# Mixing 64x64 token blocks in the corners of TensorE, with its place and the projection's last quarter reordered

## The reference

```python
# attention, last line: the heads' outputs o go through Wo
return jnp.einsum('bto,do->btd', o, Wo)

# the mixing: x is (batch, token c, feature t); w is one of eight 64x64 matrices
w = weights[subjects]
b = bias[subjects]
out = jnp.einsum('bct,bcd->bdt', x, w)
out = out + b[:, :, None]

x = x + _L2_cond_ref(...)      # x3 in the kernel
x = x + _L3_cond_ref(...)      # x4 in the kernel, the output
```

## Time and profile before

| | us |
|---|---|
| median of 3 runs | 908.46 |
| lowest and highest | 903.56, 910.40 |
| profiled execution, its own time | 904.41 |
| its span in the trace | 902.6 |

### The profile page before, as it was taken

One profiled execution on the slowest core, in us unless ns is written; L12 is line 12 of the kernel. 1 busy time (PEld: TensorE's weight loads), 2 busy tenths in 40 slices (PEclk: granted clock), 3 DMA queues, 4 the chain that ended last, 5 costly groups with the idle time before them and its releaser, 6 DMA issues. The chain is left out here.

```text
span 902.6 us, 23448 instructions
## 1 busy us (share of the span) xinstructions
PE 874.2 (97%) x6451; PEld 654.3 (72%) x6451; DVE 651.3 (72%) x1832; ACT 439.8 (49%) x1161; POOL 525.8 (58%) x496
## 2 busy tenths in 40 slices
PE   6899999999999999999996999999999999999997
PEld 4466676676767667667675788888888888888885
DVE  4664456788777855477666688888888888888885
ACT  2433333333433334333333666766667666676663
POOL 2146556566565658865558666666666666666630
PEclk9999999999999999999997999999999999999999
DMA  9999987988879788888554666666676686666741
GB/s 314 351 342 356 348 278 258 308 273 273 278 263 310 270 292 274 271 277 293 206 198 133 202 212 212 187 199 216 194 221 191 203 245 201 202 204 204 242 130 49
DMA packets 99985, 218.45 MB, mean 242 GB/s; under 512 B 29755, under 2 KB 35736, under 8 KB 91746
## 3 DMA queue, kind: packets, MB, share of 16 engines
q1 hardware_dynamic: 65858, 145.17, 48.7%
q0 software_dynamic: 25088, 57.74, 20.9%
q10 hardware_dynamic: 8992, 15.00, 4.5%
HBM read 210.29 MB, written 33.86 MB: 271 GB/s over the span
## 5 line engine op out<-in xcount | busy, mean ns | idle before, releaser
L618 POOL DMA_INDIRECT ring<-new_rows,idx x128 | 130.8, 1022 | 101.5 <-DVE big L1617 79.9
L1164 ACT ACTIVATE big<-big,neg_max 128x320 f32<-128x320 f32 x256 | 141.7, 560 | 6.3 <-DVE neg_max L1588 1.9
L1588 DVE CUSTOM_DVE_ANT_0 big<-banks,mask 128x320 f32<-128x320 f32 x256 | 114.8, 486 | 14.8 <-PE banks L878 10.8
L663 PE MATMUL banks<-ring 128*64 128x512 f32 x512 | 117.2, 600 | 3.9 <-DMA ring<-in_w 3.9
L1154 ACT ACTIVATE kt<-banks 128x384 f32<-128x384 f32 x128 | 62.6, 489 | 109.2 <-PE banks L856 109.1
L543 POOL TENSOR_TENSOR rms<-ss,neg_half 128x12 f32<-128x12 f32 x29 | 66.4, 2289 | 66.5 <-DVE ss L1494 66.5
L878 PEld LDWEIGHTS banks<-kt,q_in 64*128 64x128 f32 x768 | 75.1, 191 | 23.5 <-issue 11.6
L878 PE MATMUL banks<-kt,q_in 64*128 64x128 f32 (+2 forms) x768 | 89.0, 365 | 2.9 <-ACT kt L1154 1.3
L1617 DVE TENSOR_SCALAR big<-big,recip 128x320 f32<-128x320 f32 x256 | 84.8, 393 | 2.3
L1013 ACT ACTIVATE pair_b_hi<-pair_b,reals 128x512 fp32r<-128x512 f32 x32 | 23.2, 726 | 124.3 <-DMA pair_b<-in_lb 124.1
L541 POOL TENSOR_TENSOR ring<-ring 128x512 f32<-128x512 f32 x29 | 37.6, 1297 | 72.5 <-DVE ring L1360 72.5
(11 more groups left out here) (191 smaller groups left out, 1979.7 us busy)
## 6 DMA issues: line engine op xcount, KB each, us to landing
ring<-in_w SPq DMA_DIRECT2D x62, 1024.0 KB, 8.0
ring<-in_xt SPq DMA_DIRECT2D x32, 256.0 KB, 2.8
x_in<-in_x SPq DMA_DIRECT2D x32, 256.0 KB, 5.7
bias_in<-in_b SPq DMA_DIRECT2D x64, 128.0 KB, 8.2
x_dram<-x SPq DMA_DIRECT2D x32, 256.0 KB, 9.0
q_dram<-q_t ACTq DMA_DIRECT2D x32, 256.0 KB, 6.9
q_in<-q_dram SPq DMA_DIRECT2D x32, 256.0 KB, 2.9
x_in<-x_dram SPq DMA_DIRECT2D x32, 256.0 KB
```

What stands on the lines that cost most here:

```text
L618: pool.indirect_dma_start(out=kv[:, s, c, :], out_offset=None, in_=new_rows, in_offset=bass.IndirectOffsetOnAxis(ap=idx[:, b, 1 + c:2 + c] ...
L663: last = nc.tensor.matmul(ps_l0[T * h:T * h + T, :], xt[:, s, c, T * h:T * h + T], w0[:, 2 * s + h, c * D:(c + 1) * D], start=(c == 0), st ...
L1164: nc.scalar.activation(prob[:, s % 2, PLACE[g] * NK:(PLACE[g] + 1) * NK], sm[:, s % 2, g, :], ACT.Exp, bias=neg_max[:, s % 2, g:g + 1], sc ...
L1588: V.tensor_tensor_reduce(sm[:, s % 2, g, :], ps_s[g], mask[:, s % 2, k0:k0 + NK], 1.0, 3.0e38, ALU.add, ALU.min, accum_out=neg_max[:, s % ...
```

## The change

The mixing becomes four matmuls of 64x64 by 256 columns, one in each corner of the array: token half h of the pair (rows) times column half i. `bd` keeps one 64x64 matrix per batch, with no zeros, and DVE adds an identity to it (`join_identity`), so that the matmul gives x3 plus the mixing. DVE's `add_x4` goes; ACT adds the bias in two ACTIVATEs of 128x256 (`add_bias`), after `ot_hi` in the odd step. The four results lie in rows 64i of two banks, `ps_x` for h = 0 and the second half of bank 6 for h = 1. `mix()` moves from ahead of the values to behind `own_values()`. The projection is turned to go over chunks inside products; three chunks stay in the odd step and the last moves to the even step, ahead of the values. `add_x3` moves from the start of DVE's even step to where `add_x4` stood. For the last pair the projection begins with the high parts, before the low parts are there, and in step 64 `values(0)` is put ahead of the last `transpose_probs`. The output is stored in two DMAs for a pair, each of 64 partitions with two runs of 1 KB, and seven loads for a pair replace five (the bias goes to both halves).

```diff
+        ident_half = sb("ident_half", [P, T])
-        bd = sb("bd", [P, 2, P])
-        sbias = sb("sbias", [P, 2, 1])
+        bd = sb("bd", [P, 2, T])
+        sbias = sb("sbias", [P, 2, 2])
+        def mixed(i, h, last):
+            return (ps[2 + i][:, 0:D // 2], ps[6 + i][:, 0:D // 2])[h] if last else (ps_x[:, 0:D // 2], ps[6][:, D // 2:])[h]
...
-                        sp.wait_ge(x4_ready, k + 1 + i)
-                        sp.dma_start(a["out"][bass.ds(k, 1), :, n0:n1].rearrange("o p d -> (o p) d"), x4[:, t, n0:n1]).then_inc(st_out[t], 16)
+                        sp.wait_ge(x4_ready, k + 1 + (i if is_last(k) else 0))
+                        sp.dma_start(a["out"][bass.ds(k, 1), :, n0:n1].rearrange("o (h t) n -> (o t) h n", h=2),
+                                     x4[T * i:T * i + T, t, :].rearrange("p (h n) -> p h n", h=2)).then_inc(st_out[t], 16)
...
# TensorE, transpose_probs
+                    if odd:
+                        wait(pe, x4_ready, m - 1)
# TensorE, values
+                    ahead = isinstance(b, int) and b == NB
+                        if h == 1 and p == 1 and on(b, 4, NB):
+                            pe.wait_ge(x3_ready, pair + 1)
# TensorE, project
-                    for c in chunks:
-                        for n, (o_part, w_part) in enumerate(((ot_hi, wo_hi), (ot_hi, wo_lo), (ot_lo, wo_hi))):
+                    for n, (o_part, w_part) in enumerate(((ot_hi, wo_hi), (ot_hi, wo_lo), (ot_lo, wo_hi))):
+                        if n == 2 and is_last(pair):
+                            pe.wait_ge(ot_ready, NP)
+                        for c in chunks:
# TensorE, mix
+                        for i in columns:
+                            for h in range(2):
+                                done = nc.tensor.matmul(mixed(i, h, last)[T * i:T * i + T, :], bd[T * h:T * h + T, pair_s, :],
+                                                        x3[T * h:T * h + T, pair_s, i * D // 2:(i + 1) * D // 2], start=True, stop=True,
+                                                        skip_group_check=True)
+                        done.then_inc(l3_done, 1)
# TensorE, the order of a step
+                if isinstance(b, int) and b == NB:
+                    pe.wait_ge(ot_ready, NP - 1)
+                    values(0)
                 if on(b, 1, NB):
                     transpose_probs()
...
-                        project(range(DC), ps_x).then_inc(wo_done, 1)
+                        project(range(DC - 1), ps_x)
+                if not odd and on(b, 4, NB) and not is_last(pair):
+                    project(range(DC - 1, DC), ps_x).then_inc(wo_done, 1)
+                if not odd and on(b, 2, NB):
+                    if not (isinstance(b, int) and b == NB):
+                        values(0)
+                    values(1)
+                    own_values()
                 if not odd and on(b, 4, NB):
                     mix()
-                if not odd and on(b, 2, NB):
-                    values(0)
-                    values(1)
-                    own_values()
# ScalarE
+                def add_bias():
+                    pair, pair_s = m - 2, s // 2
+                    last = is_last(pair)
+                    wait(act, st_out[pair_s], 32 * (j - 1))
+                    act.wait_ge(ld_pair[pair_s], PAIR_DMAS * 16 * j)
+                    for part, (p0, p1) in enumerate(((0, T), (T, P)) if last else ((0, P),)):
+                        act.wait_ge(l3_done, pair + 1 + part)
+                        for i in (1, 0):
+                            done = nc.scalar.activation(x4[p0:p1, pair_s, i * D // 2:(i + 1) * D // 2], mixed(part, i, last)[p0:p1, :],
+                                                        ACT.Identity, bias=sbias[p0:p1, pair_s, i:i + 1])
+                        done.then_inc(x4_ready, 1)
                 if odd and on(b, 3, NB):
...
+                if odd and on(b, 5, NB):
+                    add_bias()
                 if on(b, -1, NB):
                     copy_keys(b + 1, s + 1, 0)
# VectorE
+                def join_identity():
+                    dve.wait_ge(ld_pair[pair_s], PAIR_DMAS * 16 * j)
+                    wait(dve, l3_done, pair - 1)
+                    V.tensor_tensor(bd[:, pair_s, :], bd[:, pair_s, :], ident_half[:, :], ALU.add)
...
-                def add_x4():
...
                 if not odd and on(b, 4, NB):
-                    add_x3()
+                    join_identity()
+                    if not on(b, 0, NB):
+                        add_x3()
...
-                if not odd and on(b, 4, NB):
-                    add_x4()
+                if not odd and on(b, 4, NB) and on(b, 0, NB):
+                    add_x3()
```

More of the change, by code:

```diff
@@ L190, in build @@
         o_view = banks[:, 4 * BANK:6 * BANK].rearrange("p (g n) -> p g n", g=GP)[:, :, 0:2 * P]
-        ps_last, ps_mix = ps[0:2], ps[2:4]
+        ps_last = ps[0:2]
+        def mixed(i, h, last):
+            return (ps[2 + i][:, 0:D // 2], ps[6 + i][:, 0:D // 2])[h] if last else (ps_x[:, 0:D // 2], ps[6][:, D // 2:])[h]
         ld_ids, ld_small, ld_ident, ld_la, ld_w1, ld_wq, ld_wkv, ld_late, ld_wo = (sem(n) for n in (
@@ L245, in build @@
         TOK_PARTS = 4
-        PAIR_DMAS = 5
+        PAIR_DMAS = 7
         def loop(eng, step, slots, first, end, last):
@@ L454, in phase_two @@
                     k, t = (b // 2 if isinstance(b, int) else j * 2 + s // 2) - 3, 1 - s // 2
-                    for i, (n0, n1) in enumerate(COLUMN_PARTS if is_last(k) else WHOLE):
-                        sp.wait_ge(x4_ready, k + 1 + i)
-                        sp.dma_start(a["out"][bass.ds(k, 1), :, n0:n1].rearrange("o p d -> (o p) d"), x4[:, t, n0:n1]).then_inc(st_out[t], 16)
+                    for i, (n0, n1) in enumerate(COLUMN_PARTS):
+                        sp.wait_ge(x4_ready, k + 1 + (i if is_last(k) else 0))
+                        sp.dma_start(a["out"][bass.ds(k, 1), :, n0:n1].rearrange("o (h t) n -> (o t) h n", h=2),
+                                     x4[T * i:T * i + T, t, :].rearrange("p (h n) -> p h n", h=2)).then_inc(st_out[t], 16)
                 if s % 2 == 0 and on(b, 2, NB):
@@ L464, in phase_two @@
                         u = sp.value_load(ids_sb[0:1, 1, bass.ds(k * 2 + h, 1)], min_val=0, max_val=NS - 1)
-                        sp.dma_start(bd[T * h:T * h + T, t, T * h:T * h + T],
+                        sp.dma_start(bd[T * h:T * h + T, t, :],
                                      a["w3"][bass.ds(u, 1)].rearrange("o c d -> (o c) d")).then_inc(ld_pair[t], 16)
-                        sp.dma_start(sbias[T * h:T * h + T, t, :],
-                                     a["b3"][bass.ds(u, 1)].rearrange("o d n -> (o d) n")).then_inc(ld_pair[t], 16)
+                        for i in range(2):
+                            sp.dma_start(sbias[T * i:T * i + T, t, h:h + 1],
+                                         a["b3"][bass.ds(u, 1)].rearrange("o d n -> (o d) n")).then_inc(ld_pair[t], 16)
             loop(sp, phase_two, 4, 8, NB + 6, NB - 4)
             for t in range(2):
-                sp.wait_ge(st_out[t], (NP // 2 + (len(COLUMN_PARTS) - 1 if t == (NP - 1) % 2 else 0)) * 16)
+                sp.wait_ge(st_out[t], NP // 2 * len(COLUMN_PARTS) * 16)
                 sp.wait_ge(st_kv[t], NP // 2 * 16)
@@ L911, in values @@
                     v = (s - 2 + h) % KV_SLOTS
[L912 to L915, removed]
+                    ahead = isinstance(b, int) and b == NB
+                    if h == 0 or ahead:
+                        pe.wait_ge(pt0_ready, b - (1 - h if ahead else 0))
+                        pe.wait_ge(pt1_ready, b - (1 - h if ahead else 0))
+                        pe.wait_ge(pt2_ready, b - (1 - h if ahead else 0))
                     for p in range(GP):
+                        if h == 1 and p == 1 and on(b, 4, NB):
+                            pe.wait_ge(x3_ready, pair + 1)
                         for c in range(2):
@@ L942, in mix @@
                 def mix():
[L944 to L948, removed]
+                    last = is_last(pair)
+                    if last:
+                        pe.wait_ge(x4_ready, pair)
+                    for part, columns in enumerate(((0,), (1,)) if last else ((0, 1),)):
+                        if last:
+                            pe.wait_ge(x3_ready, pair + 1 + part)
+                        for i in columns:
[4 more added lines that the diff above has]
+                        done.then_inc(l3_done, 1)
                 if on(b, 0, NB):
@@ L960, in phase_two @@
                 if odd and on(b, 3, NB):
-                    pe.wait_ge(ot_ready, pair + 1)
+                    if is_last(pair):
+                        pe.wait_ge(othi_ready, NP)
+                    else:
+                        pe.wait_ge(ot_ready, pair + 1)
                     if isinstance(b, int) and b == 3:
@@ L1211, in phase_two @@
                     store_queries(NP - 2, 0)
-            loop(act, phase_two, 4, 4, NB + 2, NB - 4)
```

(9 more changed lines are left out.)

## The result

The changed kernel is slower: 916.88 us (916.17 to 918.22, 4 runs) against 907.27 for the kernel before (903.56 to 910.40, 4 runs), 9.6 us by the medians; the ratio estimated from the runs is 1.0116, with a 95% interval of 1.0094 to 1.0137. The profiled execution took 918.22 us, 916.4 of them in the span.

What follows compares the result with a forecast made beforehand. PE's own work and a chain scores, DVE, ACT, keys, scores were taken to end together, both bounding the kernel. Pairs +7.8, step 4 -0.5, end -1.3 gave +6.0 us: 908.5 to 914.5, range 906 to 921.

Steps and rivals of the forecast that it cites:

- Two paths of equal length: Odd to even scores: PE's own work (4.70 us) and the chain over DVE, ACT and keys (4.69) end together.
- M: Price of the new mixing on PE, behind the own values: 0.43 us, bounds 0.43 to 0.86.
- Odd step: Own values' end to even scores: 6.42 us instead of 5.99, with PE waiting 0.70 for the keys.
- Even step: Even scores to the next own values' end: 6.44 us instead of 6.60; old mixing leaves, projection quarter comes in.
- the first step's saving: Step 4, where add_x3 is on the chain: moving it away gives at most 0.68 us, 0.5 taken.
- Cover: ACT's two new activations, 0.6 to 0.75 us, fit its idle time behind ot_hi; nothing on the path.
- Table: Rival: ACT changes its table for Identity, two loads a pair, 41 us more, 955 us; chance 0.02.
- the end: Last steps, from the last pair's normalisation through final projection and bias: together -1.3 us.
- Half of the values now lies ahead, in PE's wait: Step 64, values(0) ahead of the last transposes: costed as hidden in PE's wait, -0.95 us.
- Behind the own values the sum had -0.55: After the last own values: -0.70 us for the projection's earlier start and +0.15 for the bias activations.
- The start without the low parts: Last projection begins without waiting for the low parts: -0.70 us.
- The last bias: At the end, two ACT activations (0.26 and 0.36 us) replace one DVE operation: +0.15 us.

Runs made afterwards that it cites:

- the pair of runs with the keys first: Odd steps' second keys' copy on ACT moved ahead of the probabilities' copies: in the changed kernel 896.85 us, in the kernel before 904.68 us.
- the doubled mixing: Changed kernel with the four mixing matmuls of each pair but the last done twice into the same places: 930.5 us, ratio 1.0255.
- The first step-64 run: Changed kernel with DVE, in step 64 alone, copying the last probabilities ahead of adding x3 of pair 30: 914.24 us, run once.
- the run with the quarter back: Changed kernel with the whole projection in the odd step, its last quarter not moved to the even step: 914.36 us, ratio 1.0094.

## Why the prediction was right, and where it was not

The direction, the range and the mechanism held; the size was 6.0 forecast against 9.6 of the medians. The chances did less well: 0.64 stood on a change within 9.1 us, and the measured one lies just beyond that, where 0.26 stood.

- *Two paths of equal length.* Shown by the pair of runs with the keys first: 0.6 us a pair after the change, 0.07 before it. The 24 waits in the earlier trace rows were the sign of it; there was also a step of 1.34 for the even scores against 1.29 for the odd ones, and with the keys first in the kernel before it fell to 1.28.
- *M.* 0.43 taken, 0.43 measured, 0.86 for the doubled mixing. By an estimate from the 60 cycles that the Trainium skill gives each matmul ("TensorEngine Tiling (Array Packing)", Instruction Overhead) it would have been 0.48; the measurement decides, and here it leaves no room for them.
- *Odd step.* A stall of 0.70 forecast, 0.72 measured; 6.42 against 6.40. *Even step.* 6.44 against 6.45. A pair 12.86 against 12.85. With the first step's saving, -0.5, 7.3 was forecast from the first pair to pair 30, and 7.4 came.
- *Cover.* ACT's new work beside the path: 0.83 us, a little over the 0.75 that I had as its upper bound, in idle time, with 0.84 left. So the copies of the mixing's results out of PSUM were not the limit; the copy of the keys at the end of the chain was.
- *Table.* One table load in the changed kernel too, the 1283 ns one at the start, so the Trainium skill's sentence that identity is in every set ("ScalarE: Activation LUTs", Table sets) agrees with the trace. (The sum of that rival, 0.75 + 1.28 + 0.6, is 2.63 and not 2.65; nothing hangs on it.)
- *The step that failed* is the end: -1.3 forecast, +2.1 measured. The last own values were to end 0.7 earlier after those before, and ended 12.20 - 10.87 = 1.33 later. "Half of the values now lies ahead, in PE's wait" was costed as free, -0.95. It was not: `values(0)` needs ACT's copy of batch 62, which ACT makes behind four exponentials, at 900.64, so PE got to the last transposes at 901.98 and not at about 901.4; the run without this edit puts its worth at 0.4. And the sum has no term for a second wait: in step 64 DVE adds x3, which needs the quarter, ahead of its copy of the probabilities. I had not followed that order for this one step. PE was done with the quarter at 903.93, and `values(1)` waited until 905.30. The first step-64 run took 1.04 of it away, and the run with the quarter back 1.19. Behind the own values the sum had -0.55, and it came to +0.74. The start without the low parts came as said (0.67 behind the own values, where it was 1.47), but the projection took 3.32, where it was 3.10. The last bias was put at +0.15, for two activations. It was four of 64 rows, one behind the other, since the first half of the mixing, too, is queued behind the whole projection (907.71 + 3.32 = 911.03). They took from 911.74 to 913.43, as the end of the changed kernel's chain shows:

```profile
911.74 0.83 ACT x L1224 x2
...
913.07 0.36 ACT x L1224
```

Behind the last activation the span goes on for 2.97 us, where 2.33 followed DVE's last operation before; whether the changed stores have a part in that was not tried. Nor was it settled why the stretch up to the first pair's values is 4 us longer in one profiled execution than in another whose instructions up to there are the same.

## What to carry to other kernels

Before costing work taken off the busiest engine, find the places where it is handed something back, and measure the other path to each of them: an engine that is busy 100% of the time may be on one of two paths that end together, and then the saving counts only up to the other path's end. Moving work to a new place puts it ahead of everything that starts behind it: here 0.43 us ahead of the scores delayed a chain over three engines, while 0.44 us behind them were free. And write out the peeled first and last steps one by one; they have their own order, and a formula for the steady step does not hold there.

## What the runs showed of the hardware

- What a group of matmuls adds to the chain depends on whether PE is already running ahead of it: the same eight records in corners added 0.43 us directly behind other 64x64 work and 0.66 where PE had come to a stop, though the records themselves spanned 0.61 and 0.66. A step read from the chain holds only for a place of the same kind.
- An ACTIVATE of 128x256 with a bias from SBUF took 472 ns in the mean, longer than a copy of as many columns, which took 0.36 us in the earlier trace rows; the group by line:

```profile
L1224 ACT ACTIVATE x<-banks,sbias 128x256 f32<-128x256 f32 x62 | 26.0, 472 | 0.0
```

The Trainium skill ("ScalarE: Activation LUTs", What ACT_TABLE_LOAD costs) gives about 93 ns for each such operand; 472 - 360 = 112 is near it. The two differ in the function as well (Identity and Copy), so that the operand's part alone is not shown.
